# Two LoRA layers in one core's program: two moves in VectorE's order and one copy handed from VectorE to ScalarE

## What is computed

```python
def _L0_cond_ref(x, adapter_mapping, W, b, lora_As, lora_Bs):
    base_out = jnp.einsum('bti,oi->bto', x, W) + b
    A = lora_As[adapter_mapping]
    Bm = lora_Bs[adapter_mapping]
    lora_h = jnp.einsum('bti,bir->btr', x, A)
    lora_out = jnp.einsum('btr,bro->bto', lora_h, Bm)
    return base_out + lora_out * SCALING
...
    result = jnp.einsum('bsd,od->bso', x, base_weight) + base_bias
    A = lora_A_w[adapter_ids]
    Bw = lora_B_w[adapter_ids]
    h = jnp.einsum('bsd,brd->bsr', x, A)
    lora_out = jnp.einsum('bsr,bor->bso', h, Bw)
    result = result + lora_out
...
x = x + _L0_cond_ref(x, itok_B_0_23, L0_cond_W, L0_cond_b, L0_cond_lora_As, L0_cond_lora_Bs)
x = x + _L1_cond_ref(x, itok_B_6_15, L1_cond_base_weight, L1_cond_base_bias, L1_cond_lora_A_w, L1_cond_lora_B_w)
```

## Time and profile before

| what | value |
|---|---|
| median of 3 runs | 281.93 us (281.27 to 282.66) |
| the profiled execution's own time | 282.09 us |
| its span, first to last instruction | 280.5 us |
| TensorE matmul busy | 275.7 us, 98% |
| TensorE weight loads busy | 224.8 us, 80% |
| VectorE busy | 214.6 us, 77% |
| ScalarE busy | 101.6 us, 36% |
| GpSimd busy | 21.7 us, 8% |

### The profile page before, as it was taken

How to read it: one execution, slowest core, us unless ns; L and a number is a source line. 1 busy time by engine, 2 the same in 40 slices (tenths; PEclk the granted TensorE clock), 3 DMA queues, 4 the chain that set the end, 5 groups by cost and what they waited for, 6 DMA issues and landing times.

```text
span 280.5 us, 3865 instructions
## 1 busy us (share of the span) xinstructions
PE 275.7 (98%) x1321; PEld 224.8 (80%) x1321; DVE 214.6 (77%) x321; ACT 101.6 (36%) x141; POOL 21.7 (8%) x48
## 2 busy tenths in 40 slices
PE   8999999999999999999999999999999999999995
PEld 6888887888888885888877888888877888888885
DVE  5789999999899699898982875875772865875413
ACT  4665464352964575404231223132221223132000
POOL 3333200401002001001000000000000000000000
DMA  7997000200376200293701713702802302303003
GB/s 231 395 419 294 29 1 0 60 19 0 108 268 266 110 2 9 77 348 133 241 22 65 240 56 121 232 15 114 245 1 78 132 0 112 95 2 128 22 0 150
DMA packets 13112, 33.93 MB, mean 121 GB/s; under 512 B 2165, under 2 KB 2421, under 8 KB 13094
## 3 DMA queue, kind: packets, MB, share of 16 engines
q1 hardware_dynamic: 12066, 31.60, 31.8%
q0 software_dynamic: 1024, 2.10, 2.4%
q10 hardware_dynamic: 4, 0.00, 0.0%
HBM read 22.09 MB, written 11.60 MB: 120 GB/s over the span
## 4 chain that ended last, share of the span: by engine, by line
PE 60%; DVE 2%; issue 0%
PE bank L1305 18%; PE bank L1306 18%; PE bank L1307 18%; PE bank L1337 3%; PE bank L1312 3%; DVE ops L739 1%; PE bank L1370 0%; PE bank L1371 0%; PE bank L1369 0%; DVE ops L806 0%; DVE g_all L763 0%; DVE raw_a L808 0%; DVE raw_a L936 0%; PE bank L1372 0%; DVE aa L862 0%
## 5 line engine op out<-in xcount | busy, mean ns | idle before, releaser
L1305 PE MATMUL bank<-ops,late 128*128 128x512 f32 x192 | 75.1, 391 | 0.0
L1306 PE MATMUL bank<-ops,late 128*128 128x512 f32 x192 | 74.8, 389 | 0.0
L1307 PE MATMUL bank<-ops,late 128*128 128x512 f32 x192 | 74.7, 389 | 0.0
L1145 PE MATMUL bank<-ops 128*128 128x512 f32 x112 | 43.6, 389 | 0.0
L1146 PE MATMUL bank<-ops 128*128 128x512 f32 x112 | 43.6, 389 | 0.0
L1305 PEld LDWEIGHTS bank<-ops,late 128*128 128x128 f32 x192 | 36.0, 188 | 8.7 <-issue 1.2
L1307 PEld LDWEIGHTS bank<-ops,late 128*128 128x128 f32 x192 | 36.0, 188 | 7.6
L1306 PEld LDWEIGHTS bank<-ops,late 128*128 128x128 f32 x192 | 36.0, 188 | 7.4
L1141 PE MATMUL bank<-ops 128*128 128x512 f32 x112 | 40.7, 398 | 0.2 <-issue 0.2
L536 ACT CAST late<-rows 128x512 fp32r<-128x512 f32 x24 | 14.7, 621 | 54.6 <-DVE rows L834 29.6
L1141 PEld LDWEIGHTS bank<-ops 128*128 128x128 f32 x112 | 21.4, 192 | 5.1 <-issue 0.4
(11 more groups left out here) (177 smaller groups left out, 397.8 us busy)
## 6 DMA issues: line engine op xcount, KB each, us to landing
out<-raw_a SPq DMA_DIRECT2D x27, 256.0 KB, 2.3
raw_a<-xT SPq DMA_DIRECT2D x10, 512.0 KB, 6.6
a<-rb_rows SPq DMA_DIRECT2D x8, 392.0 KB
x_mid<-xT SPq DMA_DIRECT2D x6, 512.0 KB, 6.2
raw_b<-W SPq DMA_DIRECT2D x2, 1024.0 KB, 15.6
rb_rows<-b_hl SPq DMA_DIRECT2D x3, 512.0 KB
rb_rows<-late SPq DMA_DIRECT2D x3, 512.0 KB
raw_b<-V SPq DMA_DIRECT2D x4, 256.0 KB, 4.3
```

The lines of the kernel that those rows point to most:

```text
L1145: mm(bank[:, :], left(u, 0, k, m), op_k(v, 1, k), start=False, stop=False, skip_group_check=on_top)
L1305: mm(bank[:, :], hi, t_op(t, 0, k), start=(start and k == 0), stop=False, skip_group_check=not start)
L1306: mm(bank[:, :], hi, t_op(t, 1, k), start=False, stop=False, skip_group_check=not start)
L1307: last = mm(bank[:, :], lo, t_op(t, 0, k), start=False, stop=(k == KH - 1), skip_group_check=not start)
```

## The change

Three edits. VectorE's four `bias_first(0)` and `bias_first(1)` instructions move from ahead of `low("us4")` to just ahead of `bias_first(2)`, with their two waits. VectorE's second `g_copy` goes, and ScalarE does that copy between `high_d21(1)` and `high_d21(2)`. VectorE's `factors(0)` and `factors(1)` move ahead of `low_d21(0)`.

```diff
@@ scalar
             for n in range(KH):
                 high_d21(n)
+                if n == 1:
+
+                    act.wait_ge(g_turned, 2)
+                    nc.scalar.copy(gt_raw, b_banks[3][:, :]).then_inc(g_made, 1)
@@ vector
-            def g_copy(h):
-                dve.wait_ge(g_turned, h + 1)
-                nc.vector.tensor_copy(g_all[:, h * KH:(h + 1) * KH, :].rearrange("p k n -> p (k n)"),
-                                      (a_banks[0], b_banks[3])[h][:, :]).then_inc(g_made, 1)
+            def g_copy_first():
+                dve.wait_ge(g_turned, 1)
+                nc.vector.tensor_copy(g_all[:, 0:KH, :].rearrange("p k n -> p (k n)"), a_banks[0][:, :]
+                                      ).then_inc(g_made, 1)
@@
-            dve.wait_ge(bias1_landed, DMA)
-            dve.wait_ge(summed["vt3"], 1)
-            bias_first(0)
-            bias_first(1)
             dve.wait_ge(m1_kept, KH)
             low("us4")
             make_e1(0)
@@
-            g_copy(0)
+            g_copy_first()
             low("us2")
...
-            bias_first(2)
-            bias_first(3)
+            dve.wait_ge(bias1_landed, DMA)
+            dve.wait_ge(summed["vt3"], 1)
+            for k in range(KH):
+                bias_first(k)
             dve.wait_ge(lo[SLOT["v11"]], filled("v11", KH))
             dve.wait_ge(bias_step, 2 * KH)
             combine("vt2", "v11", "vt3", ALU.subtract)
@@
             low("t2")
-            dve.wait_ge(lo[SLOT["t3"]], filled("t3", 1))
-            low_d21(0)
-            g_copy(1)
             factors(0)
             factors(1)
-            for n in range(1, KH):
+            dve.wait_ge(lo[SLOT["t3"]], filled("t3", 1))
+            for n in range(KH):
                 low_d21(n)
```

## The result

The changed kernel takes **282.89 us** in the median of 22 runs (282.37 to 283.77), the kernel before 282.07 in as many runs beside them (281.21 to 282.92): 0.8 us slower. One run, of the version with three sums ahead and without edits 2 and 3, took 467.34 us at a granted clock of 0.56 and is left out of what is said of that version. The profiled execution of the changed kernel took 282.63 us with a span of 281.0, against 282.09 and 280.5 before.

The account below looks back on a forecast made before the run. TensorE, busy 275.7 of 280.5 us, was taken as the bound, so only its pauses count: +1.15 at G's second half and -0.51 at `h_product(0)` give +0.6 on 281.93, forecast 282.5 us, range 281.2 to 283.3.

Parts of the forecast that it names:

- the likeliest case: Whole kernel: measured time within about 0.5% (1.4 us) of the kernel before, called same, chance 0.90.
- Edit 1, start of product 3: At product 3: `low("us4")` begins 0.65 us sooner, product 3 follows the transposes at 44.03, TensorE gains 0.45 us.
- Edit 1, the lag: From `vt2` to `a_diff_lo`: VectorE 2.00 us later, G's second half then leaves TensorE 1.15 us behind.
- The tie at `s_hl`: Six matmuls around 68 us: VectorE's low part and TensorE arrive together, worth at most some 0.2 us.
- the 0.08 us that the prediction had added for the longer record: At G's second half: first matmul record after the pause is longer, 0.47 us against 0.39.
- The clock rival: At TensorE's new pause near 80 us: the array's clock falls, costing 2.0 us more, 284.5 us; chance 0.03.
- The transfers: From `t_sum` to x's split: the 2.00 us lag passes down the transfers, first split at about 96.2.
- The step "`r_bounced` comes 2.00 us later": Ahead of x's split: `t_sum` made 2.00 us later, SyncE's wait 7.3 us, so `r_bounced` comes at about 96.2.
- The rival in which the transfers slip further: From `t_sum` to `r_bounced`: transfers lose 2 us more than VectorE, ending at 284.0 us; chance 0.05.
- the gain of 0.51 us at `h_product(0)`: At `h_product(0)`: `aa` ready at 109.93, TensorE there at 110.43, so its 0.51 us pause is gone.
- both pauses: TensorE's 0.45 us ahead of product 3 and 0.5 us at `h_product(0)`: about 1 us, all that can be won.
- A small slip without consequence: At the last `low_d21` pair: the set comes 1.2 us later than before, costing nothing.

Follow-up runs that it names:

- the version with three sums ahead and without edits 2 and 3: Kernel before with only the fourth of the four bias sums moved behind `low("us4")`, second G copy and factors unmoved: 281.88 us against 281.88, ratio 1.0010.
- the later comparisons: The unaltered changed kernel run twice more beside the kernel before: 283.08 us against 281.74, and 282.87 against 281.88.
- edit 1 alone: Kernel before with only the four bias sums moved, second G copy and factors as they were: 283.77 us against 281.74, ratio 1.0074.
- the extra instruction: Changed kernel plus one unused 128x512 VectorE instruction (0.60 us) ahead of `b_sum_lo`: 283.42 us against 281.71 for the kernel before, ratio 1.0072.
- edits 2 and 3 alone: Changed kernel with the four bias sums back ahead of `low("us4")`: 281.75 us against 281.74 for the kernel before, ratio 1.0001.
- the version that removes it without a lag: Changed kernel with three of the four bias sums back ahead of `low("us4")`: 281.24 us against 281.74 for the kernel before, again 281.37 against 281.88.

## Why the prediction was right, and the term that was not

- **The median** of 282.89 lies in the range of 281.2 to 283.3, 0.4 us above the forecast of 282.5, and within 0.5% of before, as the likeliest case had it. 0.14 us of the 0.4 is the base: the forecast counts from 281.93, three runs, and the median of 22 is 282.07. The rest is a term of the sum, below. As a difference the forecast was +0.6 us; measured were +0.8 here and +1.3 and +1.0 in the later comparisons, so that the number being this near is in part luck.
- **Edit 1, start of product 3.** Idle 1.98 us ahead of `low("us4")` (1.9 forecast), product 3 earlier by 26.33 - 25.75 = 0.58 us behind O where TensorE is early enough (0.45 forecast). One step was off: the prediction has the transposes as what product 3 then waits for, 0.36 us behind the turn. In the first trace `v22`'s low part ends at 41.40 + 2.28 = 43.68, as forecast (43.73), but the turn was early, at 43.35, and product 3 still follows the low part, by the same 0.10 us as before.
- **Edit 1, the lag.** `vt2` at 56.09 (56.15 forecast), `a_diff_lo` 1.96 us late (2.00), G's second half at 81.61 (81.6), 1.21 us later than before behind O (1.15); edit 1 alone and the extra instruction show that it is VectorE's queue, one for one. The tie at `s_hl` cost 0.29 us (0.2), and was swallowed as said. Behind the new pause the next matmul comes after 0.31 us instead of 0.23, the 0.08 us that the prediction had added for the longer record.
- **The clock rival** fell: with the pause in place the granted clock stays 1.00, the level of 2.4 GHz, and the next stretch of 3 us has its 15 matmuls, as many as the earlier trace rows had without a pause. The stretch with the pause and the one behind it (the granted clock follows GpSimd's busy time):

```profile
79.00:82.00 3.00, 1.81 (x9) 1.22 (x8) 3.00 (x3) 3.00 (x3) 0.00 (x0) 1.00 0.94 325
82.00:85.00 3.00, 3.00 (x15) 2.45 (x14) 3.00 (x2) 1.62 (x3) 0.00 (x0) 1.00 0.57 187
```

  In the second and third trace of the changed kernel, and at the pause of edit 1 alone at `h_product(0)`, the granted clock stays 1.00 too. The rule of the Trainium skill that idleness lowers the clock ("TensorE: Matmul & The Clock Gate", Part 1) is not contradicted; a pause of this length did not bring it about in any trace here.
- **The transfers.** x's first split was forecast at 96.2 and came at 95.51. The step "`r_bounced` comes 2.00 us later" took `t_sum`'s transfer as fixed at 7.3 us of waiting; here it was 6.6. The rival in which the transfers slip further did not occur. ScalarE's new copy ended at 106.1 us (estimate 107), ahead of `low("t2")`'s end at 108.8, and kept nobody waiting.
- **Mis-sized: the gain of 0.51 us at `h_product(0)`.** It was read from a single trace, in which the wait stood, and it depends on that same transfer. Between that trace and the first of the changed kernel the gain is there in full, and more: 3.37 - 2.71 = 0.66 us. The prediction had TensorE ready for `h_product(0)` 1.00 us behind the start of the bias row's sum (109.28 - 108.28, with 0.09 us estimated). In the four traces that wait there it begins 1.51, 1.35, 2.25 and 1.70 us behind it (the last two are edit 1 alone and three ahead without edits 2 and 3), and p1 comes 0.66, 0.51, 1.41 and 0.85 us later than 2.71, so TensorE was ready after 0.84 to 0.85 us. But two of four traces of the kernel before have no such wait, and edits 2 and 3 alone moved the median by nothing. Against those two, p1 of the changed kernel is 94.17 - 92.9 = 1.3 us late, against the two others 0.7: the medians' 0.8, 1.3 and 1.0 us lie in this span. The 1.3 belongs to the comparison in which edits 2 and 3 alone gained nothing; both would follow if the kernel before mostly had no wait there, which its untraced runs do not tell.
- The prediction also called both pauses "about 1 us together, all that the change can win". By the table product 3 begins 26.3 to 26.4 us behind O in every trace of before, whether TensorE was there 0.7 us earlier or only just then (the second trace). This start is set by VectorE, and in the changed kernel it still is, at 25.75, in two of three traces. It was the dependable one of the two terms: the version that removes it without a lag gains its 0.5 us, with edits 2 and 3 in place.
- A small slip without consequence: the last `low_d21` pair was put 1.2 us later than before. By the prediction's own terms it is 2.00 - 0.60 = 1.4; measured, its second instruction begins at 113.48 instead of 112.91, 0.6 us later, since x came less late than forecast.

## What to carry over

Before work is moved out of the way of a late step, see whether its engine would wait there for another anyway: only the part of the moved work that sticks out of that idle time wins anything, and whatever is moved beyond it comes back as lag where the next consumer has less slack. Here four instructions stuck out by one; with edits 2 and 3, moving one gave 0.5 us, and moving four lost 0.8 to 1.3. And a pause read in one trace is a sample: if it hangs on a transfer, take a second trace, and compare times from a common origin, not from the start.

## What the runs showed of the hardware

- The transfer of `t_sum`, 0.5 KB out to DRAM, kept SyncE waiting for 6.3 to 7.4 us in these traces, with values at both ends for the same kernel (6.5, 6.6, 7.2 and 7.3 in the four of before). That spread of 0.8 us goes on to what follows: x's first split, which waits for SyncE's later transfers, lies 75.15 to 76.01 us behind O in the same four traces.
- The loads at the start move the whole program: O lay between 17.91 and 19.94 us. Where VectorE sets the pace behind O, a late TensorE does not show in the time: in the changed kernel product 3 began at 25.75 or at 26.59 us behind O, and p1 at 94.16 both times.
- Pauses of TensorE of 0.94 to 1.34 us behind product 6, whose 48 matmuls run 0.227 us apart, left the granted clock at 1.00. Each cost its own length and 0.07 to 0.08 us more, since the second matmul behind it came after 0.30 to 0.31 us.
